# A decoder layer on one core: the weights' rounding in pieces of 768 columns, one to a batch, and single operations on x placed one step apart

## The chip, the cores and the metric

The kernel runs on one core of one Trainium2 chip. The core has five engines, each with its own queue of instructions that it works off in order: PE (TensorE, matrix products and transposes), DVE (VectorE), ACT (ScalarE), POOL (GpSimd) and SP (SyncE, which here only issues DMAs). The engines wait for one another by semaphores that are written out in the kernel. The metric is the device time of one execution in microseconds (us), as the median of three.

## The reference

One decoder layer over x of 16 batches x 256 rows x 512 columns, in three parts that each normalise x and add to it:

```python
x = x + attention(layernorm(x), w_qkv, w_proj)       # 16 heads of 32, causal
x = x + mixing(layernorm(x), k, bias, ctx, ctx, 8)   # long convolution along the 512 columns
x = x + ffn(layernorm(x), gate_w, up_w, down_w, ...) # 512 -> 1536 -> 512, silu(gate) * up

def bitlinear(x, w):       # in attention, for q, k, v and for the output
    xq = round(x * 127 / rowmax(|x|)), clipped to -128..127, times rowmax(|x|) / 127
    wq = round(w / mean(|w|)), clipped to -1..1, times mean(|w|)
    return xq @ wq.T

def quantized_matmul(x, w, scale):   # in the ffn
    return (x @ w.astype(float8_e4m3fn).astype(float32)) * scale
```

The change lies in the attention and in the rounding of gate_w and up_w (each 512 x 1536) to the values of the 8-bit format.

## The kernel before

The program has two parts. Part 1 does the attention of all 16 batches and writes x + attention to a scratch tensor in memory; beside it, it rounds gate_w and up_w and writes them as float16 to another one, `wq8_dram`. Part 2 does mixing and ffn, and is not touched but for the form in which it reads `wq8_dram`. It starts when both scratch tensors are complete (`part1_done`).

Part 1 has no planner. Each engine's program runs one loop over the same **steps** t (`STEPS`, from -13 to 153), and in a step it issues what `pair`, `batches`, `project_steps`, `halves` and `weight_step` give for that t. A step takes one **pair** of heads: 8 pairs to a batch (`PAIRS`), so a batch takes 8 steps, and everything that a batch needs once comes back every 8 steps. This text calls t mod 8 the **phase** of a step. In step t there are:

- PE: `weigh` of pair t-12 (probabilities times v), `row_max` of pair t (scores into the PSUM tile `s_qk`), `probabilities` of pair t-8 (scores, turned, into `s_kq`), and once or more a batch `turn_oq`, `project_out`, `multiply_qk`, `multiply_v`, `turn_xq`, `spread_c`, `turn_max`;
- DVE: `take_max` of pair t-1 (maxima from `s_qk`, tile blockmax), and the rest of a batch: scaling of q and k (`qkt`), splitting of v (`vHL`), norm statistics, row maxima, `finish`;
- ACT: `weighed` of pair t-13 (tile oraw), `exponentials` of pair t-9 (pT), `high_part` of pair t-10 (pH, the float16 rounding; at phase 2 DVE does it), and a batch's normalising, rounding, copies and diagonals;
- POOL: `low_part` of pair t-11 (pL), `low_qk`, small things, and two of the four operations on a piece of weights.

`s_qk` and `s_kq` exist once, so `row_max` of pair t waits for `take_max` of pair t-1, and `probabilities` waits for the exponentials of the pair before. pT and pH have three buffers, pL two. The results of all other products go to three PSUM banks in turn (`misc1`, class `Banks`): who takes a bank waits until the one taken three before has been released.

What a batch needs once is placed by numbers: `batches(t, FINISH, 13)` gives k = 0 at phase 5, and k = 4 (phase 1) rounds both halves of the output `o_sb` on ACT, k = 5, 6 turn them on PE, k = 6, 7 copy them on ACT, k = 9, 11 project them on PE (phases 6 and 0), k = 10, 12 add them to x on DVE (phases 7 and 1). `batches(t, NORM_AT, ...)` with k = LOAD_AHEAD + j falls on phase j: x is normalised at 3, both halves rounded and both diagonals `diag` made at 6, all turned by PE at 7, all copied by ACT (`xqT`) at 0, and the diagonals' product copied (`cbc`) at 2.

A **piece** of weights is 128 rows x 512 columns, 24 in all. Its chain: SP loads it (fw_raw), DVE masks the exponent's bits out of it (fw_pow) and clamps that from below, ACT scales fw_pow, POOL adds fw_pow to fw_raw and later subtracts it again (fw_out, float16), SP stores fw_out. It is placed by a list of its own with a period of five steps:

```python
weight_steps = {t: i for i, t in enumerate(t for t in STEPS if t >= 0 and t % 5 < 2)}
```

so at t mod 5 = 1 DVE has mask and clamp and POOL the subtraction for the piece before, at t mod 5 = 0 POOL has the addition, and ACT scales two steps behind DVE. Phases and weights thus meet in a pattern that comes back every 40 steps.

Of the kernel before, what the change touches and what calls it, by code (L numbers as in the profile page):

```python
# [5 lines left out]
F32 = mybir.dt.float32  # L6
# [7 lines left out]
P = 128  # L14
# [52 lines left out]
def decoder_kernel(nc, x, skip, ctx_in, w_qkv, w_proj, k_turned, w_gate, w_up, w_down,  # L67
# [18 lines left out]
    PIECE = 512  # L86
# [4 lines left out]
    with ExitStack() as ctx:  # L91
# [18 lines left out]
        wmax = sb(ctx, "wmax", [P, 2, CB * INNER // PIECE], F32)  # L110
# [143 lines left out]
        fw_in, fw_stored = signals("fw_in", 3), signals("fw_stored", 2)  # L254
        fw_pow_done, fw_scaled, fw_added, fw_taken = signal("fw_pow"), signal("fw_scaled"), signal("fw_added"), signal("fw_taken")
# [27 lines left out]

        def pair(t, lag):
            n = t - lag
            return n if 0 <= n < B * PAIRS else None
# [24 lines left out]
        def weight_step(t):  # L311
            k = weight_steps.get(t)
            return k if k is not None and k < W_STEPS else None

        W_REST = range(min(len(weight_steps), W_STEPS), W_STEPS)

# [34 lines left out]
        def part1_done(w):  # L351

            for t in range(NT):
                x1_stored(w, t)
            for n in range(PIECES - 2, PIECES):
                w.wait_ge(fw_stored[n % 2], 16 * (n // 2 + 1))
            w.wait_ge(fw_pow_done, PIECES)
            w.wait_ge(fw_taken, PIECES)
# [32 lines left out]
        def tensor_program(tensor):  # L391
# [27 lines left out]
            def turn_xq(b):  # L419
                w.wait_ge(xround_done, b + 1)  # L420
                for j in range(2):
                    bank = misc1.take(("xqT", b, j), w, (xqT_done, 2 * b + j + 1))
                    for i in range(2):
                        cb = 2 * j + i
                        for t in range(NT):
                            made = T.transpose(bank[:, i * N + t * P:i * N + (t + 1) * P], xn[:, t, cb * P:(cb + 1) * P], ident[:])
                    made.then_inc(xqT_pe, 1)
# [86 lines left out]
            def turn_oq(b, j):  # L514
                w.wait_ge(o_round, b + 1)
# [26 lines left out]
            turn_xq(0)  # L542
# [7 lines left out]
            turn_xq(1)  # L550
# [4 lines left out]
            for t in STEPS:  # L555
# [6 lines left out]
                for b, k in batches(t, FINISH, 13):  # L562
                    if k in (5, 6):
                        turn_oq(b, k - 5)
                    if k in (9, 11):
                        project_out(b, (k - 9) // 2)
                for b, k in project_steps(t):
                    if k < 4:
                        multiply_qk(b, k)
                    elif k in (PAIRS + 5, PAIRS + 7):  # L570
                        multiply_v(b, (k - PAIRS - 5) // 2)
                for b, k in batches(t, NORM_AT, 11 + LOAD_AHEAD, 2):
                    if k == LOAD_AHEAD + 7:
                        turn_xq(b)
# [131 lines left out]
        def vector_program(vector):  # L706
# [109 lines left out]
            def finish(b, k):  # L816
# [23 lines left out]
                elif k in (10, 12):  # L840
                    t, xs = (k - 10) // 2, x_sb[b % NX]
# [5 lines left out]
            def weight_pieces(k):  # L847
                if k == 0:
                    return
                n, second = divmod(k - 1, 2)  # L850
                if not second and n < PIECES:

                    raw, pw = fw_raw[n % 3], fw_pow[n % 2]
                    wT_ready(w, 3)
                    w.wait_ge(fw_in[n % 3], 16 * (n // 3 + 1))
                    if n >= 2:
                        w.wait_ge(fw_taken, n - 1)
                    m, at = divmod(n, PIECES // 2)
# [927 lines left out]
```

## Time and profile before

| | before |
|---|---|
| time, median of 3 executions (lowest, highest) | 1638.09 us (1636.88, 1639.48) |
| the profiled execution: its time, its span | 1636.98 us, 1635.2 us |
| share of the span busy: PE, DVE, ACT, POOL | 91%, 78%, 43%, 61% |
| first and last `take_max` of part 1 (DVE) | 67.25 and 480.82 us |
| last addition to x in part 1 (DVE) | starts at 518.82 us |
| first work on part 2's x (DVE) | starts at 523.86 us |

The span goes from the first to the last instruction in the profile of one execution; the 1.8 us between it and that execution's time lie outside. Busy shares over the whole span mix two parts with different limits, so they say little on part 1. What happens in part 1 is read in windows of time, and a step's length is the distance from one `take_max` on DVE (line 790) to the next, since each step has exactly one.

### The profile page before, as it was taken

The page shows a single profiled execution, that of the slowest core. Times are in us where ns is not written, and L with a number is a line of the kernel's source. Part 1 is how long each engine was busy: PE and PEld are TensorE (multiplying, and loading weights), DVE is VectorE, ACT ScalarE, POOL GpSimd, SP SyncE. Part 2 cuts the span into 40 slices and gives each one's busy share as a digit, 9 for nine tenths or more (in the row PEclk, how much of TensorE's full clock was granted, in tenths as well). Part 3 has the DMA queues.
Part 4 walks back from the last instruction along what each step waited for, and adds up shares of the span by engine and source line. Part 5 has one row for each costly group of instructions (what it writes and reads, how often), then busy time and mean ns, then how long its engine had stood idle before and what let it go on. Part 6 is the DMA issues. An engine that isn't in the chain of part 4 may idle for free.

```text
span 1635.2 us, 24145 instructions
## 1 busy us (share of the span) xinstructions
PE 1492.7 (91%) x9045; PEld 841.9 (51%) x9045; DVE 1280.3 (78%) x1865; ACT 698.3 (43%) x1230; POOL 993.3 (61%) x722
## 2 busy tenths in 40 slices
PE   2589898988985978899999999999999999999998
PEld 2477777777763433444444444444444444444443
DVE  6689898999874879887788788878887878778621
ACT  4589898988884102322222222232223222222131
POOL 2379898998883366754664546645654565465242
PEclk9799999999997989999999999999999999999999
DMA  3544645454423322000200210030020020010010
GB/s 132 153 123 130 159 123 139 137 142 124 130 83 105 95 65 77 20 26 7 72 25 2 55 43 7 20 78 7 13 78 14 8 71 26 2 45 0 1 27 26
DMA packets 62036, 105.79 MB, mean 65 GB/s; under 512 B 7880, under 2 KB 14176, under 8 KB 61920
## 3 DMA queue, kind: packets, MB, share of 16 engines
q1 hardware_dynamic: 61728, 104.10, 23.4%
q8 instruction: 72, 1.18, 0.3%
q14 instruction: 44, 0.36, 0.1%
q10 hardware_dynamic: 192, 0.14, 0.1%
HBM read 50.74 MB, written 19.92 MB: 43 GB/s over the span
## 4 chain that ended last, share of the span: by engine, by line
PE 60%; DVE 4%; POOL 2%; issue 1%; ACT 0%; POOLq 0%; DVEq 0%
PE gu L663 20%; PE y L628 10%; PE gu L677 10%; PE y L631 3%; PE y L635 3%; PE y L632 3%; PE y L634 3%; PE y L636 3%; PE gu L616 3%; PE misc L643 1%; PE misc L653 1%; PE misc L592 1%; PE misc L536 1%; DVE z L975 1%; DVE oT L986 1%
## 5 line engine op out<-in xcount | busy, mean ns | idle before, releaser
L1548 POOL TENSOR_TENSOR fuL<-fu,fuH 128x512 f16<-128x512 f32 x96 | 125.1, 1303 | 248.1 <-ACT fuH L1355 248.1
L628 PE MATMUL y<-kv,toep 128*128 128x512 f32 x496 | 242.8, 612 | 19.9 <-DVE z L975 17.7
L1450 POOL TENSOR_TENSOR pL<-pT,pH 128x768 f16<-128x768 f32 x128 | 220.5, 1725 | 42.5 <-ACT pH L1197 25.7
L986 DVE TENSOR_REDUCE oT<-z 128x64 f32<-128x512 f32 x256 | 175.7, 686 | 8.8
L663 PE MATMUL gu<-fT,wg 128*128 128x512 f16 x768 | 181.5, 379 | 0.4 <-ACT fT L1374 0.4
L663 PE MATMUL gu<-fT,wu 128*128 128x512 f16 x768 | 181.4, 379 | 0.0
L982 DVE TENSOR_TENSOR z<-z,cT 128x512 f32<-128x512 f32 x112 | 168.0, 1500 | 3.8
L1355 ACT ACTIVATE fuH<-fu 128x512 f16<-128x512 f32 x96 | 60.2, 627 | 255.1 <-DVE fu L1001 255.1
L979 DVE TENSOR_TENSOR z<-y,shared 128x512 f32<-128x512 f32 x112 | 76.9, 687 | 90.8 <-PE y L632 76.9
L677 PE MATMUL gu<-wd,fuL 128*128 128x512 f16 x384 | 145.6, 379 | 0.0
L677 PE MATMUL gu<-wd,fuH 128*128 128x512 f16 x384 | 145.6, 379 | 0.0
L628 PEld LDWEIGHTS y<-kv,toep 128*128 128x128 f32 x496 | 92.8, 195 | 101.3 <-issue 62.0
L1516 POOL TENSOR_TENSOR kv<-vT,cT 128x1024 f32<-128x1024 f32 x64 | 138.5, 2183 | 5.5 <-ACT vT L1332 5.5
L1191 ACT ACTIVATE pT<-s_kq,ws 128x768 f32<-128x768 f32 x128 | 114.9, 898 | 51.9 <-PE s_kq L493 46.9
L663 PEld LDWEIGHTS gu<-fT,wg 128*128 128x128 f16 x768 | 75.1, 98 | 119.4 <-issue 47.1
L663 PEld LDWEIGHTS gu<-fT,wu 128*128 128x128 f16 x768 | 75.2, 98 | 106.4 <-issue 35.4
L790 DVE TENSOR_REDUCE blockmax<-s_qk 128x6 f32<-128x768 f32 x128 | 121.5, 949 | 9.8 <-PE s_qk L463 9.5
L975 DVE TENSOR_TENSOR z<-y,cT 128x512 f32<-128x512 f32 x144 | 98.4, 683 | 29.5 <-PE y L628 29.3
L1338 ACT ACTIVATE shared<-gu 128x512 f32<-128x512 f32 x56 | 33.4, 597 | 204.1 <-PE gu L616 204.1
L1443 POOL TENSOR_TENSOR qkhl<-qkt,qkhl 128x512 f16<-128x512 f32 x64 | 81.7, 1279 | 38.5 <-ACT qkhl L1177 38.5
L479 PE MATMUL s_kq<-pack 128*128 128x128 f16 x768 | 99.7, 220 | 0.0
L1001 DVE SCALAR_TENSOR_TENSOR fu<-gu,cols,sil 128x512 f32<-128x512 f32 x96 | 71.3, 743 | 33.6 <-PE gu L663 33.6
(188 smaller groups left out, 3433.9 us busy)
## 6 DMA issues: line engine op xcount, KB each, us to landing
pack<-qkhl SPq DMA_DIRECT2D x256, 128.0 KB, 2.5
x_sb<-in_x SPq DMA_DIRECT2D x16, 512.0 KB, 4.9
c_sb<-in_ctx SPq DMA_DIRECT2D x32, 256.0 KB, 4.6
hankel<-in_L_xattn_k SPq DMA_DIRECT2D x32, 256.0 KB, 4.2
x_grp<-x_scratch SPq DMA_DIRECT2D x32, 256.0 KB, 4.0
out_y<-yo SPq DMA_DIRECT2D x32, 256.0 KB, 2.9
x_scratch<-x_sb SPq DMA_DIRECT2D x15, 512.0 KB, 2.8
wraw<-in_L_attn_w_qkv SPq DMA_DIRECT2D x3, 1024.0 KB, 9.7
```

Source lines behind the costliest of these rows:

```text
L479: T.matmul(to, pack[:, 1, r, g, key * P:(key + 1) * P], pack[:, 0, r, g, query * P:(query + 1) * P], start=first, stop=False)
L628: made = T.matmul(to, tap(h, lb - kb), keys_values(h, kb, half), start=kb == 0, stop=kb == lb)
L663: made = T.matmul(bank[:], (wg, wu)[which][:, cb, ib * P:(ib + 1) * P], fT[:, cb, part, :], start=cb == 0 and part == 0, stop=cb == CB - 1 ...
L677: made = T.matmul(bank[:], src[:, ib, t * P:(t + 1) * P], wd[:, ib, :], start=ib == 0 and part == 0, stop=ib == IB - 1 and part == 1)
L790: V.tensor_reduce(out=blockmax[b % 2][:, p, :], in_=s_qk[:, 0:6, :], op=ALU.max, axis=AXIS.X, negate=True).then_inc(max_done, 1)
L975: V.tensor_tensor(z[n % 2][:], y, weight, ALU.mult).then_inc(m_zm, 1)
L982: chain.step(V.tensor_tensor(z[n % 2][:], z[n % 2][:], weight, ALU.mult))
L986: V.tensor_reduce(out=oT[h % 2][:, lb, own].rearrange("p (b j) -> p b j", b=HB), in_=z[n % 2][:], op=ALU.add, axis=AXIS.X).then_inc(m_z, 1)
L1191: S.activation(pT[n % NP][:], s_kq[:, 0:6, :], ACT.Exp, scale=ws[:, 4:5]).then_inc(exp_done, 1)
L1450: G.tensor_tensor(pL[n % 2][:], pT[n % NP][:], pH[n % NP][:], ALU.subtract).then_inc(low_done, 1)
L1516: G.tensor_tensor(kv[LB * (h % 2) + lb][:], vT[h % 2][:, lb, :].rearrange("p (b i) -> p b i", b=B).unsqueeze(2).broadcast_to([P, B, M_POS, ...
L1548: G.tensor_tensor(fuL[:, ib, :], fu[n % 2][:], fuH[:, ib, :], ALU.subtract).then_inc(f_fl, 1)
```

## The change

The pieces become 768 columns wide and 16 in number, one to a batch, and `weight_steps` goes: piece n is masked at t = 8n + 2, clamped at 8n + 3, scaled at 8n + 4, added at 8n + 11, subtracted at 8n + 12 and stored at 8n + 13, where piece n + 2 is loaded too. The mask and the clamp are joined by a semaphore of their own (`fw_mask`) and no longer by the chain inside one step. fw_raw has two buffers for three, fw_out one for two.

The operations on x that stood two in a step stand one in a step: the output's rounding at k = 4, 5, its turning at 6, 7, the copies at 7, 8, projecting at 10, 11, the addition to x at 11, 12; x's rounding at phases 6 and 7, its turning at 0 and 1, the copies at 1 and 2, the diagonals at 0. The number of these operations is the same; the signals `o_round` and `xround_done` count halves now.

```diff
-    PIECE = 512
+    PIECE = 768
...
-        fw_raw = [q(f"fw_raw{i}", [P, PIECE], F32) for i in range(3)]
+        fw_raw = [q(f"fw_raw{i}", [P, PIECE], F32) for i in range(2)]
...
-        fw_out = [q(f"fw_out{i}", [P, PIECE], F16) for i in range(2)]
+        fw_out = q("fw_out", [P, PIECE], F16)
...
+        OUT_ROUND_AT, OUT_TURN_AT, OUT_COPY_AT, OUT_AT, X1_AT = (4, 5), (6, 7), (7, 8), (10, 11), (11, 12)
+
+        X_ROUND_AT, X_TURN_AT, X_COPY_AT = (6, 7), (8, 9), (9, 10)
+
+        V_AT, V_SPLIT_AT = (13, 15), (14, 16)
...
-        weight_steps = {t: i for i, t in enumerate(t for t in STEPS if t >= 0 and t % 5 < 2)}
-        W_STEPS = 1 + 2 * (PIECES + 1)
...
+        MASK_AT, CLAMP_AT, FACTOR_AT, ADD_AT, TAKE_AT, STORE_AT = 2, 3, 4, 11, 12, 13
+
+        def piece(t, at):
+            n, k = divmod(t - at, PAIRS)
+            return n if k == 0 and 0 <= n < PIECES else None
...
-            def turn_xq(b):
-                w.wait_ge(xround_done, b + 1)
-                for j in range(2):
...
+            def turn_xq(b, j):
+                w.wait_ge(xround_done, NT * (b + 1))
...
-                for b, k in batches(t, FINISH, 13):
-                    if k in (5, 6):
-                        turn_oq(b, k - 5)
-                    if k in (9, 11):
-                        project_out(b, (k - 9) // 2)
+                for b, k in batches(t, FINISH, 14):
+                    if k in OUT_TURN_AT:
+                        turn_oq(b, OUT_TURN_AT.index(k))
+                    if k in OUT_AT:
+                        project_out(b, OUT_AT.index(k))
...
-                elif k in (10, 12):
-                    t, xs = (k - 10) // 2, x_sb[b % NX]
+                elif k in X1_AT:
+                    t, xs = X1_AT.index(k), x_sb[b % NX]
...
-            def weight_pieces(k):
...
+            def mask_piece(n):
+                wT_ready(w, 3)
+                w.wait_ge(fw_in[n % 2], 16 * (n // 2 + 1))
+                if n >= 2:
+                    w.wait_ge(fw_taken, n - 1)
+                V.tensor_scalar(fw_pow[n % 2][:].bitcast(I32), fw_raw[n % 2][:].bitcast(I32), EXPONENT, None,
+                                ALU.bitwise_and).then_inc(fw_mask, 1)
...
+            def take_piece(n):
+                w.wait_ge(fw_added, n + 1)
+                if n > 0:
+                    w.wait_ge(fw_stored, 16 * n)
+                G.tensor_tensor(fw_out[:], fw_raw[n % 2][:], fw_pow[n % 2][:], ALU.subtract).then_inc(fw_taken, 1)
...
-                    elif k == LOAD_AHEAD + 6:
-                        round_in(b)
-                    elif k == LOAD_AHEAD + 8:
-                        copy_xqT(b)
...
+                    for i in range(NT):
+                        if k == LOAD_AHEAD + X_ROUND_AT[i]:
+                            round_in(b, i)
+                    if k == LOAD_AHEAD + 8:
+                        diagonal(b)
+                    for j in range(2):
+                        if k == LOAD_AHEAD + X_COPY_AT[j]:
+                            copy_xqT(b, j)
...
+                if (n := piece(t, STORE_AT)) is not None:
+                    store_piece(n)
+                    load_piece(n + 2)
```

**ACT at phases 6 and 7** of a full batch, in the order of its queue. oraw opens a step; xn is the rounding of x, qkhl the high half of q and k, nmT the turned maxima. Before, in a batch where the weights' list meets phase 6:

```order
L1205 ACTIVATE oraw<-pv 128x2x130
L1191 ACTIVATE pT<-s_kq,ws 128x768
L1197 ACTIVATE pH<-pT 128x768
L1177 ACTIVATE qkhl<-qkt 128x512
L1137 ACTIVATE xn<-xn,small 128x512 x2
L1142 ACTIVATE diag<-ident,small 128x128 x2
L1184 ACTIVATE nmT<-misc 32x256
L1236 ACTIVATE fw_pow<-fw_pow 128x512
L1205 ACTIVATE oraw<-pv 128x2x130
L1191 ACTIVATE pT<-s_kq,ws 128x768
L1197 ACTIVATE pH<-pT 128x768
L1177 ACTIVATE qkhl<-qkt 128x512
```

The same two steps of the changed kernel (its line numbers are 6 to 10 higher):

```order
L1214 ACTIVATE oraw<-pv 128x2x130
L1200 ACTIVATE pT<-s_kq,ws 128x768
L1206 ACTIVATE pH<-pT 128x768
L1186 ACTIVATE qkhl<-qkt 128x512
L1143 ACTIVATE xn<-xn,small 128x512
L1193 ACTIVATE nmT<-misc 32x256
L1214 ACTIVATE oraw<-pv 128x2x130
L1200 ACTIVATE pT<-s_kq,ws 128x768
L1206 ACTIVATE pH<-pT 128x768
L1186 ACTIVATE qkhl<-qkt 128x512
L1143 ACTIVATE xn<-xn,small 128x512
```

One rounding has moved to phase 7, the diagonals to phase 0, the weights' scaling (which met phase 6 here by its period of five) to phase 4.

**ACT at phase 2**, with the end of phase 1 before it. osmall is a batch's output scale, cbc the spread scale of x. Before:

```order
L1218 ACTIVATE o_sb<-o_sb,osmall 128x512 x2
L1223 ACTIVATE osmall<-osmall,ws 128x2
L1113 ACTIVATE small<-small 128x2
L1114 ACTIVATE small<-small 128x2
L1205 ACTIVATE oraw<-pv 128x2x130
L1191 ACTIVATE pT<-s_kq,ws 128x768
L1149 ACTIVATE cbc<-misc 128x256
L1184 ACTIVATE nmT<-misc 32x256
```

The changed kernel, phase 2 alone:

```order
L1214 ACTIVATE oraw<-pv 128x2x130
L1200 ACTIVATE pT<-s_kq,ws 128x768
L1227 ACTIVATE o_sb<-o_sb,osmall 128x512
L1232 ACTIVATE osmall<-osmall,ws 128x2
L1166 ACTIVATE xqT<-misc 128x512
L1159 ACTIVATE cbc<-misc 128x256
L1193 ACTIVATE nmT<-misc 32x256
```

One rounding of the output, its scale and one copy of turned x have come into the step; the copy of the maxima nmT stands behind them.

**DVE at phases 1 and 2** (and 3). x_sb is the addition to x. Before, in a batch where the weights' list meets phase 1:

```order
L790 TENSOR_REDUCE blockmax<-s_qk 128x6
L844 SCALAR_TENSOR_TENSOR x_sb<-misc,osmall,x_sb 128x512
L780 TENSOR_SCALAR vHL<-misc,small 128x16x32
L783 SCALAR_TENSOR_TENSOR vHL<-misc,small,vHL 128x16x32
L859 TENSOR_SCALAR fw_pow<-fw_raw 128x512
L861 TENSOR_SCALAR fw_pow,wmax<-fw_pow 128x512
L790 TENSOR_REDUCE blockmax<-s_qk 128x6
L814 CAST pH<-pT 128x768
```

The changed kernel, phases 1 to 3 of every batch that has a piece:

```order
L800 TENSOR_REDUCE blockmax<-s_qk 128x6
L854 SCALAR_TENSOR_TENSOR x_sb<-misc,osmall,x_sb 128x512
L790 TENSOR_SCALAR vHL<-misc,small 128x16x32
L793 SCALAR_TENSOR_TENSOR vHL<-misc,small,vHL 128x16x32
L800 TENSOR_REDUCE blockmax<-s_qk 128x6
L824 CAST pH<-pT 128x768
L862 TENSOR_SCALAR fw_pow<-fw_raw 128x768
L800 TENSOR_REDUCE blockmax<-s_qk 128x6
L818 TENSOR_TENSOR nmT<-misc,nmT 32x256
L790 TENSOR_SCALAR vHL<-misc,small 128x16x32
L793 SCALAR_TENSOR_TENSOR vHL<-misc,small,vHL 128x16x32
L869 TENSOR_SCALAR fw_pow,wmax<-fw_pow 128x768
```

The mask stands behind the cast at phase 2 and the clamp a step later. The other addition to x, which stood at phase 7, stands at phase 0.

## Rows read from the trace of the kernel before

**Rows 1.** Stage windows: us, then each engine's busy us, clock, DMA share, GB/s.

```profile
490.00:545.00 55.00, 34.31 (x217) 18.14 (x218) 27.28 (x37) 21.86 (x40) 25.98 (x17) 0.78 0.49 144
```

**Rows 2.** Windows in part 1: PE, PEld, DVE, ACT, POOL busy, in this order.

```profile
162.12:300.65 138.53, 125.21 (x1521) 102.32 (x1520) 125.10 (x207) 123.16 (x244) 124.55 (x92) 0.99 0.52 138
274.90:300.65 25.75, 24.30 (x305) 20.14 (x304) 24.05 (x45) 24.13 (x49) 23.68 (x18) 1.00 0.56 155
241.10:247.06 5.96, 4.44 (x53) 3.06 (x51) 5.43 (x13) 5.96 (x13) 5.96 (x5) 1.00 0.00 1
```

**Rows 3.** Timeline of DVE, four starts of a step: start us, length us.

```profile
136.32 0.95 DVE L790 TENSOR_REDUCE blockmax<-s_qk 128x6 f32<-128x768 f32 x1
162.12 0.95 DVE L790 TENSOR_REDUCE blockmax<-s_qk 128x6 f32<-128x768 f32 x1
300.65 0.95 DVE L790 TENSOR_REDUCE blockmax<-s_qk 128x6 f32<-128x768 f32 x1
385.60 0.95 DVE L790 TENSOR_REDUCE blockmax<-s_qk 128x6 f32<-128x768 f32 x1
```

**Rows 4.** Groups by form in 162.12 to 300.65: busy, mean ns, idle before.

```profile
L1450 POOL TENSOR_TENSOR pL<-pT,pH 128x768 f16<-128x768 f32 x40 | 69.1, 1730 | 13.6 <-ACT pH L1197 8.4 <-PE pv L511 5.1
L790 DVE TENSOR_REDUCE blockmax<-s_qk 128x6 f32<-128x768 f32 x41 | 38.9, 949 | 2.0 <-PE s_qk L463 2.0
L1191 ACT ACTIVATE pT<-s_kq,ws 128x768 f32<-128x768 f32 x41 | 36.8, 897 | 15.9 <-PE s_kq L493 14.4 <-POOL pL L1450 1.2
L1197 ACT ACTIVATE pH<-pT 128x768 f16<-128x768 f32 x35 | 29.3, 838 | 0.0
L1443 POOL TENSOR_TENSOR qkhl<-qkt,qkhl 128x512 f16<-128x512 f32 x21 | 27.2, 1295 | 0.0
...
L1127 ACT ACTIVATE xn<-x_sb,small 128x512 f32<-128x512 f32 x10 | 7.6, 810 | 0.0
...
L844 DVE SCALAR_TENSOR_TENSOR x_sb<-misc,osmall,x_sb 128x512 f32<-128x512 f32 x10 | 7.5, 747 | 0.2
...
L1218 ACT ACTIVATE o_sb<-o_sb,osmall 128x512 f32<-128x512 f32 x10 | 6.6, 715 | 0.0
L1137 ACT ACTIVATE xn<-xn,small 128x512 f32<-128x512 f32 x10 | 6.6, 713 | 0.0
...
L1157 ACT ACTIVATE xqT<-misc 128x512 bf16<-128x512 f32 x10 | 5.3, 576 | 0.0
...
L808 DVE TENSOR_TENSOR nmT<-misc,nmT 32x256 bf16<-32x256 f32 x10 | 4.1, 413 | 2.2 <-ACT nmT L1184 2.0
...
L1142 ACT ACTIVATE diag<-ident,small 128x128 f32<-128x128 f32 x10 | 3.4, 390 | 0.0
```

**Rows 5.** The weights' operations, same view and window.

```profile
L1466 POOL TENSOR_TENSOR fw_out<-fw_raw,fw_pow 128x512 f16<-128x512 f32 x8 | 10.8, 1354 | 0.0
L1469 POOL TENSOR_TENSOR fw_raw<-fw_raw,fw_pow 128x512 f32<-128x512 f32 x8 | 10.2, 1271 | 0.0
L859 DVE TENSOR_SCALAR fw_pow<-fw_raw 128x512 int32<-128x512 int32 x8 | 8.5, 1062 | 0.0
...
L861 DVE TENSOR_SCALAR_CACHE_REDUCE fw_pow<-fw_pow 128x512 f32<-128x512 f32 x8 | 5.5, 686 | 0.3
...
L1236 ACT ACTIVATE fw_pow<-fw_pow 128x512 f32<-128x512 f32 x8 | 5.0, 622 | 0.0
```

**Rows 6.** Timeline of all engines at 244.44 to 244.52.

```profile
244.47 1.94 DVE L859 TENSOR_SCALAR fw_pow<-fw_raw 128x512 int32<-128x512 int32 x1
244.49 1.64 POOL L1450 TENSOR_TENSOR pL<-pT,pH 128x768 f16<-128x768 f32 x1
```

**Rows 7.** The mask's line over the whole run: ns min/median/max.

```profile
L859 DVE TENSOR_SCALAR fw_pow<-fw_raw x24: 414/903/1951, 70.1 to 448.7; 128x512 int32<-128x512 int32 x24
```

**Rows 8.** Timeline of PE, two neighbours of four products each.

```profile
300.26 1.03 PE L528 MATMUL misc<-wprojT,oqT 128*128 128x512 bf16 x4
301.12 1.03 PE L446 MATMUL misc<-wqkvT,xqT 128*128 128x512 bf16 x4
```

More of the change, by code:

```diff
@@ L549, in tensor_program @@
             spread_c(1)
-            turn_xq(1)
+            for j in range(2):
+                turn_xq(1, j)
             bank = misc1.take("tab", w, (tab_done, 1))
@@ L569, in tensor_program @@
                         multiply_qk(b, k)
[L570 to L574, printed above, removed]
+                    elif k in V_AT:
+                        multiply_v(b, V_AT.index(k))
+                for b, k in batches(t, NORM_AT, LOAD_AHEAD + 11, 2):
+                    for j in range(2):
+                        if k == LOAD_AHEAD + X_TURN_AT[j]:
+                            turn_xq(b, j)
                     if k == LOAD_AHEAD + 9:
@@ L845, in finish, with clamp_piece @@
                                            in1=xs[:, t, :], op0=ALU.mult, op1=ALU.add).then_inc(x1_done, 1)
-            def weight_pieces(k):
[L848 to L858, printed above, removed]
-                    chain.step(V.tensor_scalar(pw[:].bitcast(I32), raw[:].bitcast(I32), EXPONENT, None, ALU.bitwise_and))
-                    chain.wait()
-                    V.tensor_scalar(pw[:], pw[:], FP8_MIN_NORMAL, None, ALU.max, ALU.max,
-                                    accum_out=wmax[:, m, at:at + 1]).then_inc(fw_pow_done, 1)
+            def mask_piece(n):
[5 more added lines that the diff above has]
+                                ALU.bitwise_and).then_inc(fw_mask, 1)
+            def clamp_piece(n):
+                m, at = divmod(n, PIECES // 2)
+                w.wait_ge(fw_mask, n + 1)
+                V.tensor_scalar(fw_pow[n % 2][:], fw_pow[n % 2][:], FP8_MIN_NORMAL, None, ALU.max, ALU.max,
+                                accum_out=wmax[:, m, at:at + 1]).then_inc(fw_pow_done, 1)
             stats_in(0)
@@ L902, in vector_program @@
                     high_part(n)
-                for b, k in batches(t, FINISH, 13):
+                for b, k in batches(t, FINISH, 14):
                     finish(b, k)
@@ L919, in vector_program @@
                         join_max(use)
-                if (k := weight_step(t)) is not None:
-                    weight_pieces(k)
-            for k in W_REST:
-                weight_pieces(k)
+                if (n := piece(t, MASK_AT)) is not None:
+                    mask_piece(n)
+                if (n := piece(t, CLAMP_AT)) is not None:
+                    clamp_piece(n)
             scored(w)
@@ L1261, in scalar_program @@
             copy_c(0)
-            copy_xqT(0)
+            for j in range(2):
+                copy_xqT(0, j)
             copy_weights(1)
@@ L1271, in scalar_program @@
             step_in(1)
-            round_in(1)
+            for i in range(NT):
+                round_in(1, i)
+            diagonal(1)
             copy_weights(3)
             copy_c(1)
-            copy_xqT(1)
+            for j in range(2):
+                copy_xqT(1, j)
             for t in STEPS:
@@ L1283, in scalar_program @@
                     high_part(n)
-                for b, k in batches(t, FINISH, 13):
+                for b, k in batches(t, FINISH, 14):
                     finish(b, k)
@@ L1304, in scalar_program @@
                         high_max(use)
-                if (k := weight_step(t - 2)) is not None and k > 0:
-                    weight_pieces(k)
+                if (n := piece(t, FACTOR_AT)) is not None:
+                    scale_piece(n)
                 if t == PREFETCHED_AT:
@@ L1681, in sync_program @@
             for t in STEPS:
-                for b, k in batches(t, FINISH, 13):
-                    if b == B - 1 and k in (10, 12):
-                        store_half((k - 10) // 2)
-                    elif k == 12:
+                for b, k in batches(t, FINISH, 14):
+                    if b == B - 1 and k in X1_AT:
+                        store_half(X1_AT.index(k))
+                    elif k == X1_AT[1]:
                         store_x1(b)
```

158 lines of the change are left out of this document (67 added, 91 removed).

## The prediction

> **What bounds the kernel now.** Part 2 is the same instructions in both kernels, so I read part 1. In the stage windows of steady state [rows 2] 40 steps, one full period of phases and weights, take 138.53 us, and no engine is the bound by itself: PE is busy 125.2, DVE 125.1, POOL 124.6, ACT 123.2 us. The two starts 40 steps apart [rows 3] say the same: a batch of 8 steps lasts 27.7 us and holds 25.0 us of each engine. The missing 2.7 us are waits that go round: the groups with idle time before them [rows 4] show pL on POOL waiting for ACT and PE (13.6 us), pT on ACT for PE (15.9), and each is the first instruction of its step. The reason is in the code: one `s_qk`, one `s_kq` and three pT let no engine run more than about a step ahead of another. So a step lasts about as long as its busiest engine, and it is not always the same one. The window of one step, 241.10 to 247.06 [rows 2], took 5.96 us with ACT and POOL busy throughout, where a mean step takes 3.46.
>
> **Loads by phase.** I added the durations of what each engine has in each phase, from the groups by form [rows 4, 5] and their neighbours in that view. Instructions overlap a little with the next (the groups' sums exceed the busy time of [rows 2]); I took off 0.09 us each on ACT, 0.06 on DVE, 0.045 on POOL. For PE the two neighbours [rows 8] start 0.86 us apart: I took 0.9 for each product of a batch of this size (v, projecting, one of four for q and k), 0.5 for four transposes, and 1.8 for the three things of every step as the rest. An example, ACT phase 6: pT 0.897, pH 0.838, oraw 0.375, qkhl 0.621, roundings 2 x 0.713, diagonals 2 x 0.390, nmT 0.358 make 5.30, less 9 x 0.09 is 4.49, and a fifth of the weights' scaling (0.53) makes 4.59. Without a rounding and the diagonals it is 3.26. Us per step, before > after, weights spread over the phases before and in their places after:
>
> | phase | DVE | ACT | POOL | PE |
> |---|---|---|---|---|
> | 0 | 3.09 > 3.44 | 3.55 > 3.07 | 3.44 > 2.94 | 3.6 > 4.1 |
> | 1 | 3.30 > 2.96 | 3.69 > 3.25 | 3.44 > 2.94 | 2.7 > 3.2 |
> | 2 | 1.93 > 2.78 | 1.76 > 2.96 | 3.22 > 2.71 | 3.2 > 2.7 |
> | 3 | 2.97 > 3.60 | 3.89 > 3.28 | 2.19 > 3.34 | 3.2 > 3.2 |
> | 4 | 3.25 > 2.91 | 2.45 > 3.10 | 2.19 > 3.37 | 2.7 > 3.2 |
> | 5 | 3.17 > 2.83 | 2.60 > 3.00 | 3.35 > 2.84 | 3.0 > 3.0 |
> | 6 | 3.29 > 2.95 | 4.59 > 3.26 | 3.44 > 2.94 | 3.6 > 2.7 |
> | 7 | 4.05 > 3.02 | 2.48 > 2.99 | 3.44 > 2.94 | 2.8 > 2.7 |
> | batch | 25.0 > 24.5 | 25.0 > 24.9 | 24.7 > 24.0 | 24.8 > 24.8 |
>
> The batch sums before lie within 0.4 us of a fifth of [rows 2].
>
> **The change part by part.** (1) *Pieces of 768*: 24 become 16 with the same columns. From [rows 5], POOL pays 24 x (1.354 + 1.271) = 63.0 us before; 768 columns in the same form cost 1.73 (pL in [rows 4]), so 16 x (1.73 + 1.70) = 54.9 after. The scaling on ACT goes from 24 x 0.53 to 16 x 0.75 (pH, 768 columns, 0.838 less overlap): 12.8 to 12.0. The clamp goes from 0.69 + 0.08 to 0.96 + 0.08 (256 columns more, at the 0.27 us by which pT exceeds qkhl). (2) *The mask* is the unknown. It takes 0.414 to 1.951 us, mean 1.06 [rows 5, 7]; it took 1.94 where POOL began its pL 0.02 us later [rows 6]. Alone, 768 columns cost 0.414 x 1.5 = 0.62; behind one whole pL 0.62 + 1.73 = 2.35. I keep the mean's excess (0.65) and take 1.26. (3) *The moves* cost nothing in busy time: the same ten of each form in five batches [rows 4]. What is late next: q and k need both xqT copies, now at phases 1 and 2 before `multiply_qk` at 3; the second addition stays at phase 1; x's load and store keep their steps. (4) *Banks*: I followed the takes. Before, v at phase 0 waited for ACT's copy that ends phase 0 and v at 2 for cbc that ends ACT's phase 2; after, cbc's product at phase 1 waits for DVE's v split that ends its phase 1 (2.96 us), where PE stands at 1.8 + 0.5, and v at phase 2 for the second xqT copy. Waits of some tenths on both sides; I charge none. (5) *SP* issues 32 DMAs for pieces instead of 48, at a phase with no packing of q and k, and a load has five steps (16 us) to land. With 0.52 of the DMA engines' time used [rows 2] nothing is late. Two raw buffers serve as well as three: a piece is subtracted (phase 4) one step before its buffer is loaded again.
>
> A rule of the Trainium skill bears on (2). SBUF — State Buffer, section "Who interferes with whom", says that VectorE's `tensor_scalar` and cast in their two-port mode and any GpSimd instruction exclude each other for a whole instruction. [Rows 6] agree: the mask ends 0.28 us after POOL's pL does. By that rule, with POOL busy 93% of the time after, a mask would wait half a POOL instruction nearly always, some 1.4 us for 1.26: 2 us more in 16 pieces.
>
> **The sum.** If every step took its busiest engine, a batch would take 31.0 us before (over the 40 steps, weights in place) and 26.6 after. If the slack is one step, the busiest mean of two neighbouring steps counts: 28.35 before, 26.06 after. Measured are 27.7, which is 0.80 of the way from the bare 25.04 to 28.35. The same place after is 24.90 + 0.80 x 1.16 = 25.8. Nine full batches stand between the starts at 136.32 and 385.60 [rows 3], 249.3 us: 9 x (27.70 - 25.83) = 16.8 us. The other seven lack parts of the work and spread less badly; I give them 0.45 us each, 3 us. The drain at the end of part 1 (PE busy 34 of 55 us [rows 1]) is a chain of single operations of the last batch, in which two roundings in one step or two make no difference, and the last piece is stored at step 133, before x's last addition at 153: 0. Together 20 us: 1637.0 becomes 1617.0, and since the median of the runs stands 1.1 us above the profiled execution, 1618.
>
> That the even batch is near the truth shows in the trace: the batch from 274.90 to 300.65 has the same work and 1.6 pieces like the others, and took 25.75 us [rows 2].
>
> **Rivals.** *Waits take the place (0.17).* ACT's phase 2 grows from 1.76 to 2.96 and its nmT copy stands last; DVE's L808 at phase 3 needs it and already waits 2.0 us for it in ten [rows 4]. PE's phase 0 becomes the longest of all, 4.1 for 3.6. If 0.6 and 0.5 us come on top, a batch takes 26.9: 9 x 0.8 + 2 = 9 us, 1629. Against it: at phase 7, where ACT's phase 6 was 4.59, the same wait gets shorter.
> *Nearly no waits left (0.12).* A batch at the bare 24.9: 9 x 2.8 + 6 = 31 us, 1607. The 2.7 us that are lost now speak against all of it going.
> *Only the saved instruction time counts (0.05).* If the waits come from latency between engines and not from uneven steps, and PE's unchanged sum carries on: 1638. The even batch of 25.75 speaks against it.
> *Slower (0.06).* Cast and mask both stand in DVE's phase 2. If each waits for a whole pL, phase 2 is 0.89 + 2 x 2.29 = 5.5 us for 2.8. Its two pairs with phases 1 and 3 rise by 1.1 and 1.4, a batch takes 28.3, and the nine are 5 us slower: 1643. It decides from about 4.9 us in that phase on. For it: masks of 1.94 occur. Against: that is the largest of 24, the median is 0.90. The skill's rule above makes it possible, since it lets a whole instruction block; it doesn't say how often.
>
> **How the numbers follow.** The forecast, 25.1 to 26.7 us a batch and so 1611 to 1627, has 0.60. Below it lies 1607 with 0.12, above it 1629 (0.17), 1638 (0.05), 1643 (0.06). The range 1607 to 1632 leaves out about half of the second case and all of the last two, 0.2 in all. Within 0.2% (3.3 us, what three executions can tell from no change) is the case of 1638 and a corner of 1629: faster 0.88, same 0.06, slower 0.06.
>
> **What would show it.** Forty steps from a `take_max` in the middle of part 1 take 129 us, and all batches from the fourth on take the same time within 0.3 us, with no step above 4.3 us. Part 1's last addition to x begins near 499, and from there to the end nothing changes by more than 1 us. The mask's mean is 1.1 to 1.5 us in 16 instances. ACT's pT waits for PE fall to a half. I am wrong if a batch stays above 26.9 us though steps are even (latency), if L808 waits over 0.5 us a time, or if the mask's mean exceeds 2 us.

## The result, and the profile after

The changed kernel takes 1601.74 us in the median of four executions (1601.21 to 1602.39), the kernel before 1637.49 us beside it. The ratio is 0.978, with a 95% interval of 0.9763 to 0.9797: 2.2% or 36 us faster. The forecast of 1618 had the direction, but its range (1607 to 1632) ended above the time.

The page of the changed kernel, for its span, its busy times and slices (the profiled execution took 1601.21 us):

```profile
span 1599.4 us, 23982 instructions
...
PE 1479.1 (92%) x8967; PEld 839.6 (52%) x9045; DVE 1261.7 (79%) x1841; ACT 697.4 (44%) x1222; POOL 992.7 (62%) x706
...
POOL 2389999999973477456545654655645654566242
```

POOL shows nine tenths and more in every slice from the fourth to the eleventh, and part 1 ends 35 us earlier, not quite a slice of 40 us. The windows that answer to [rows 2], the first over batches 3 to 11 (72 steps from the `take_max` of pair 24 to that of pair 96), the second over 40 steps:

```profile
131.16:355.02 223.86, 219.16 (x2692) 181.84 (x2735) 210.63 (x352) 219.06 (x433) 221.83 (x154) 1.00 0.55 150
205.78:330.21 124.43, 122.17 (x1497) 101.11 (x1521) 116.51 (x198) 121.52 (x241) 122.94 (x86) 1.00 0.55 152
```

These nine batches took 249.28 us before [rows 3] and take 223.86 now: 27.70 us a batch, then 24.87. Busy time per batch fell by 1.7 us on DVE and by 0.3 to 0.6 us on the others, and most of the idle time went: POOL is busy 98.8% of the 40 steps, where it was busy 90%. (A small part of the fall is less work in the window: 40 steps hold 3840 columns of weights now, 5 x 768, and held 8 x 512 = 4096.) The groups by form in the 40 steps, to be read against [rows 4] and [rows 5]:

```profile
L1465 POOL TENSOR_TENSOR pL<-pT,pH 128x768 f16<-128x768 f32 x41 | 68.3, 1666 | 1.1 <-PE pv L518 0.7
...
L1200 ACT ACTIVATE pT<-s_kq,ws 128x768 f32<-128x768 f32 x41 | 36.8, 897 | 2.9 <-PE s_kq L500 2.5
...
L1480 POOL TENSOR_TENSOR fw_out<-fw_raw,fw_pow 128x768 f16<-128x768 f32 x5 | 9.1, 1824 | 0.0
L1474 POOL TENSOR_TENSOR fw_raw<-fw_raw,fw_pow 128x768 f32<-128x768 f32 x5 | 9.1, 1819 | 0.0
...
L818 DVE TENSOR_TENSOR nmT<-misc,nmT 32x256 bf16<-32x256 f32 x10 | 4.1, 414 | 0.3
...
L862 DVE TENSOR_SCALAR fw_pow<-fw_raw 128x768 int32<-128x768 int32 x5 | 2.8, 554 | 0.0
```

pL's idle time before it is 1.1 us where it was 13.6, pT's 2.9 where it was 15.9. The row that stands out is the last: the mask of 768 columns takes 0.554 us, about half of what the mask of 512 columns took on average. Over the whole run it is the same (min, median, max):

```profile
L862 DVE TENSOR_SCALAR fw_pow<-fw_raw x16: 546/554/556, 68.8 to 430.6; 128x768 int32<-128x768 int32 x16
```

Batches 4 to 11 take 24.81 to 25.14 us each, with nearly the same eight step lengths every time, from 2.0 us (phase 2) to 4.1 us (phase 3). So the batches became even, the steps did not, but the longest of before had 5.96 us [rows 2].

Of the 35.8 us between the spans, 25.4 are these nine batches, 7.7 the others up to the last `take_max` (164.3 us before, 156.6 now), 1.6 lie ahead of the first `take_max`, and 1.1 behind the last one.

### The profile page after: what moved, and what is told of

It is laid out like the page before. It is cut to its first block, busy times and chain, and to the rows that moved or that the text cites. A ratio compares the mean times of both kernels' runs of the same rounds, so it can differ in the third digit from the quotient of the medians.

```text
span 1599.4 us, 23982 instructions
## 1 busy us (share of the span) xinstructions
PE 1479.1 (92%) x8967; PEld 839.6 (52%) x9045; DVE 1261.7 (79%) x1841; ACT 697.4 (44%) x1222; POOL 992.7 (62%) x706
## 4 chain that ended last, share of the span: by engine, by line
PE 61%; DVE 4%; POOL 2%; issue 1%; ACT 0%; POOLq 0%; DVEq 0%
PE gu L673 21%; PE y L638 10%; PE gu L687 10%; PE y L641 3%; PE y L646 3%; PE y L642 3%; PE gu L626 3%; PE y L645 3%; PE y L644 3%; PE misc L663 1%; PE misc L602 1%; PE misc L653 1%; PE misc L543 1%; DVE z L983 1%; DVE oT L994 1%
## 5 line engine op out<-in xcount | busy, mean ns | idle before, releaser
L1465 POOL TENSOR_TENSOR pL<-pT,pH 128x768 f16<-128x768 f32 x128 | 216.6, 1694 | 10.9 <-ACT pH L1206 4.7
L1370 ACT ACTIVATE fuH<-fu 128x512 f16<-128x512 f32 x96 | 60.3, 628 | 254.8 <-DVE fu L1009 254.8
L1458 POOL TENSOR_TENSOR qkhl<-qkt,qkhl 128x512 f16<-128x512 f32 x64 | 85.9, 1345 | 41.1 <-ACT qkhl L1186 41.1
```

The source lines that it names most:

```text
L1465: G.tensor_tensor(pL[n % 2][:], pT[n % NP][:], pH[n % NP][:], ALU.subtract).then_inc(low_done, 1)
```

## The experiments

Times of whole kernels scatter more from one series of executions to the next than within one: the changed kernel alone gave 1601.7 and then 1606.4 us. Its nine batches took 223.86 and 223.84 us. The difference lies behind the last `take_max`: from there to the end it is 1153.3 us in one profile and 1159.4 in the other, and 4.7 of these 6.1 us fall in the drain of part 1, up to the end of the last addition to x (38.3 and 43.0 us, at a granted clock of 0.87 and 0.73). Over all kernels here the drain takes 36 to 43 us and the rest of the span, part 2 with its start, 1114 to 1118. So I compare batches 3 to 11 (the window from pair 24 to pair 96, divided by nine) and give the time beside it. Each ratio is to executions of the kernel before that were taken with it.

The nine batches do not hold the same share of the weights in every kernel: 15 pieces of 512 or 10 of 768 (7680 columns) in before, x_only and period7, and 9 of 768 (6912 columns) in the kernels with a piece to a batch. So the table also has the time from the first to the last `take_max`, in which all pieces of all kernels lie.

| kernel | us, median | ratio (95%) | us a batch | first to last `take_max`, us | mask median us |
|---|---|---|---|---|---|
| before | 1637.49 | 1 | 27.70 | 413.6 | 0.90 |
| x_only | 1626.93 | 0.9932 (0.9914 to 0.9951) | 27.23 | 405.9 | 0.80 |
| period7 | 1623.45 | 0.9909 (0.9891 to 0.9927) | 27.00 | 404.1 | 0.97 |
| before_nomask | 1618.15 | 0.9878 (0.9863 to 0.9892) | 26.07 | 393.6 | none |
| pool_heavy | 1617.07 | 0.9866 (0.9849 to 0.9883) | 26.04 | 394.8 | 2.00 |
| period7_nomask | 1611.96 | 0.9838 (0.9822 to 0.9855) | 25.95 | 392.7 | none |
| pool_heavy_nomask | 1608.30 | 0.9826 (0.9809 to 0.9843) | 25.65 | 387.4 | none |
| mask_shift | 1611.12 | 0.9840 (0.9826 to 0.9855) | 25.30 | 388.1 | 0.76 |
| sum_on_dve | 1611.49 | 0.9844 (0.9829 to 0.9859) | 25.23 | 386.9 | 0.55 |
| no_add | 1602.83 | 0.9787 (0.9768 to 0.9806) | 25.19 | 383.0 | 0.55 |
| add_on_dve | 1609.15 | 0.9821 (0.9799 to 0.9843) | 25.17 | 386.4 | 0.55 |
| weights_only | 1612.12 | 0.9844 (0.9826 to 0.9863) | 25.15 | 385.9 | 0.55 |
| the changed kernel | 1601.74 | 0.978 (0.9763 to 0.9797) | 24.87 | 380.5 | 0.55 |
| after_again | 1606.39 | 0.9804 (0.9785 to 0.9823) | 24.87 | 380.9 | 0.55 |
| clamp_at_2 | 1603.50 | 0.9787 (0.9773 to 0.9802) | 24.87 | 379.7 | 0.55 |
| nomask | 1603.01 | 0.9792 (0.9775 to 0.9808) | 24.78 | 379.7 | none |
| no_scale | 1604.47 | 0.9797 (0.9778 to 0.9816) | 24.77 | 381.0 | 0.55 |

### The two halves of the change

weights_only puts the operations on x back:

```diff
-        OUT_ROUND_AT, OUT_TURN_AT, OUT_COPY_AT, OUT_AT, X1_AT = (4, 5), (6, 7), (7, 8), (10, 11), (11, 12)
-        X_ROUND_AT, X_TURN_AT, X_COPY_AT = (6, 7), (8, 9), (9, 10)
+        OUT_ROUND_AT, OUT_TURN_AT, OUT_COPY_AT, OUT_AT, X1_AT = (4, 4), (5, 6), (6, 7), (9, 11), (10, 12)
+        X_ROUND_AT, X_TURN_AT, X_COPY_AT = (6, 6), (7, 7), (8, 8)
...
-                    if k == LOAD_AHEAD + 8:
+                    if k == LOAD_AHEAD + 6:
                         diagonal(b)
```

> The changed kernel with the output's and x's roundings, turns, copies, diagonals and additions put back to their old steps; the weights stay in pieces of 768, one to a batch. Theory A (a step lasts as long as its busiest engine, averaged over two neighbouring steps, and what made the batch long was mostly the weights landing on steps that were already full): by the loads of the steps a full batch holds 26.4 us by pairs of steps, against 28.35 before and 26.1 in the changed kernel, so this kernel keeps nearly all of the gain: 25.0 to 25.6 us a batch, 1602 to 1612 us. Theory B (the two halves of the change are independent and each levels its own part): about half of the gain, 1616 to 1624 us, batches of 26.3 us.

x_only keeps those moves and has the weights' code and list of before (`PIECE = 512`, `weight_steps`, three and two buffers).

> The changed kernel with the weights as before (24 pieces of 512 columns, by the list with a period of five steps), and only the operations on x spread. Theory A: by pairs of steps a batch holds 28.4 us, as before, because pieces still land on full steps; 27.3 to 28 us a batch, 1630 to 1640 us, and steps of 5 us and more are still there. Theory B: half of the gain, 1616 to 1624 us.

Measured: weights_only 25.15 us a batch, x_only 27.23. Theory B falls: the weights carry 2.55 of the 2.83 us. Theory A was right on where the gain lies and a little off on x_only (its range began at 27.3 us and 1630), which gains 0.47 us a batch where it expected next to nothing. From the other side x's part is 25.15 - 24.87 = 0.28. Together the halves make 3.02, so they are nearly additive. From the first to the last `take_max` it is the same picture: 27.7 us for the weights and 7.7 for x, of 33.1.

### Place or size of the pieces

period7 has the pieces of the change every seven steps:

```diff
-        MASK_AT, CLAMP_AT, FACTOR_AT, ADD_AT, TAKE_AT, STORE_AT = 2, 3, 4, 11, 12, 13
+        MASK_AT, CLAMP_AT, FACTOR_AT, ADD_AT, TAKE_AT, STORE_AT = 2, 3, 4, 6, 7, 8
...
-            n, k = divmod(t - at, PAIRS)
+            n, k = divmod(t - at, 7)
```

> The changed kernel with its 16 pieces of 768 columns placed every 7 steps instead of every 8 (mask, clamp, scaling, addition, subtraction and store at 2, 3, 4, 6, 7, 8 of 7n), so that the pieces sweep over all phases of a batch. Size and number of the pieces are those of the change, only the place is not. Theory A (the place pays): a batch holds 28.8 us by pairs of steps, so most of the gain is lost, 26.8 to 28 us a batch on average with a pattern of 7 batches, 1622 to 1640 us, and the mask's mean is near 1.1 us again since it meets POOL's long instructions. Theory C (fewer and larger instructions pay): batches stay near 25 us, 1602 to 1608 us.

Measured: 27.00 us, within theory A's range; the mask has its long instances again (0.547 to 1.997 us). Size and number alone are worth 27.23 - 27.00 = 0.2 us a batch, the place 27.00 - 24.87 = 2.1. A part of the 2.1 is the tenth piece that period7 has in these nine batches, but the time from the first to the last `take_max`, with all pieces of each kernel in it, says the same: 1.9 us for size and number, 23.6 for the place. Theory C falls.

pool_heavy moves POOL's two operations to phases with a low half of q and k (`ADD_AT, TAKE_AT = 8, 9`).

> The changed kernel with POOL's addition and subtraction at phases 0 and 1, where POOL has a low half of q and k beside pL, instead of 3 and 4, where it has pL alone. Nothing else moves. Theory A: POOL's steps 0 and 1 hold 4.7 us, a batch 28.0 us by pairs of steps; 26 to 27.5 us a batch, 1615 to 1635 us. Theory D (POOL is the bound by its sum, 24.6 us busy of a batch's 24.8, and the place doesn't matter as long as the period is 8): 24.8 to 25.2 us a batch, 1601 to 1606 us.

Measured: 26.04 us, at the lower end of theory A's; D falls. But the reason is not only the full POOL steps, since the mask rose to a median of 2.0 us, at most 2.18. At 294.05 us it stands for 2.00 us, and POOL's pL began at 293.67 and took 1.96: POOL is now in a long instruction when the mask comes.

### The mask

To part the two I left out the mask, in four kernels. They round gate_w and up_w to other values, so they serve for the time alone:

```diff
-                V.tensor_scalar(fw_pow[n % 2][:].bitcast(I32), fw_raw[n % 2][:].bitcast(I32), EXPONENT, None,
-                                ALU.bitwise_and).then_inc(fw_mask, 1)
...
-                w.wait_ge(fw_mask, n + 1)
-                V.tensor_scalar(fw_pow[n % 2][:], fw_pow[n % 2][:], FP8_MIN_NORMAL, ...
+                V.tensor_scalar(fw_pow[n % 2][:], fw_raw[n % 2][:], FP8_MIN_NORMAL, ...
```

> The changed kernel without the mask; the clamp reads the raw piece instead. It leaves out the masking of the exponent, so the rounding of the gate and up weights is another. Control for the next kernel. DVE has 0.5 us less in phase 2 and is not the bound: theories E, G, H all expect 24.8 us a batch, 1599 to 1603 us.

> The kernel with POOL's addition and subtraction at phases 0 and 1, and without the mask (it leaves out the masking of the exponent, so the rounding of the gate and up weights is another). Theory A (two full POOL steps of 4.7 us cost what they exceed the others by): about 26 us a batch as with the mask, 1612 to 1617 us. Theory G (what cost there was the mask of 2.0 us, and the cast, held up by POOL in phase 2): 24.8 to 25.3 us a batch, 1601 to 1606 us. Both with the cast held up (0.3 us) as before.

Measured: nomask 24.78, pool_heavy_nomask 25.65. With the mask, the two differ by 1.17 us, without it by 0.87. So about three quarters of pool_heavy's loss stay without the mask, and a quarter is the mask. Theory G's 24.8 to 25.3 was too low, A's 26 too high. That the three quarters are all POOL's full steps is not shown: the cast at phase 2 takes 1.04 us in the median of pool_heavy_nomask and 0.55 in nomask, so a part of the 0.87 can be the cast held up.

> The kernel before without the masks of its 24 pieces (it leaves out the masking of the exponent, so the rounding of the gate and up weights is another). Theory G+ (what made the batches of before long was mainly DVE held up by POOL in the masks, 1.06 us each in the mean for 0.41 alone): 26.0 to 26.5 us a batch for 27.7, 1613 to 1623 us. Theory A (pieces that land on full steps of ACT and POOL, the mask being one part): the mask's own 1.5 x 1.0 us a batch is partly on the path: 26.8 to 27.3 us, 1624 to 1634 us.

This one decides the share in the kernel before. Its nine batches, 26.07 us each, and the first lines of the waits in them:

```profile
134.67:369.26 234.59, 222.68 (x2736) 180.73 (x2733) 212.34 (x354) 221.23 (x439) 225.84 (x166) 1.00 0.55 145
```

```profile
PEld s_qk L458 <- DVE blockmax L790: 9.7, 17, 1.0
PEld pv L510 <- issue: 9.6, 20, 0.8
ACT pT L1189 <- PE s_kq L493: 9.5, 14, 1.6
```

The batch falls by 1.63 us, the range of G+. The nine batches of before hold 15 masks of 17.5 us in all, 1.94 us a batch (a mean of 1.17; the 1.06 of [rows 5] is that of eight). So in the kernel before a mask cost 0.98 us on the path, five sixths of its length, hold-up included, though no engine was the bound by its sum. From the first to the last `take_max` it is the same: 20.0 us for 24 masks of 24.1 us. The same in period7_nomask:

> The kernel with pieces of 768 columns every 7 steps, without the masks (it leaves out the masking of the exponent, so the rounding of the gate and up weights is another). With masks its batches took 27.0 us. Theory G+: 25.0 to 25.5 us, 1605 to 1610 us. Theory A: 26.3 to 26.8 us, 1616 to 1622 us.

Measured 25.95 us, between both theories: 1.05 us less than period7, and 1.17 more than nomask at the regular place. From the first to the last `take_max` the two differences are 11.3 and 13.0 us. The second is the price of the irregular place with no mask in it; which operations collide there was not tried one by one.

mask_shift moves the mask one step ahead (`MASK_AT = 1`).

> The changed kernel with the mask of a piece at phase 1 instead of phase 2, behind the split of v; all else stays. At phase 2 POOL has only two small operations beside pL, at phase 1 pL and a low half. Theory G (the mask's 0.55 us in the changed kernel come from its place beside POOL's small operations; beside long ones it is held up): mask mean 1.2 to 2.2 us in 16, as in the kernel with POOL's work at phases 0 and 1 (median 2.0); DVE has 1.2 us to spare in a batch, so a batch gets 0.2 to 1.2 us longer, 1605 to 1618 us. Theory H (the mask is short because of its size and number): it stays 0.55 us and the time 1600 to 1603 us.

Measured: 25.30 us, in G's range of loss, but its reason fell for the most part: the mask's mean over all 16 is 0.92 us, not above 1.2. Four of them are long (1.95, 1.72, 1.70, 1.07, in the first full batch and the last three); the others take 0.55 to 0.77. What the waits show in the nine batches is another thing:

```profile
ACT pT L1200 <- PE s_kq L500: 8.9, 17, 1.2
PEld s_qk L465 <- DVE blockmax L800: 6.7, 18, 1.2
POOL pL L1465 <- DVE pH L824: 5.6, 9, 1.0
```

At phase 2 DVE makes the pH that POOL's pL needs. The mask ahead of it makes DVE's phase 1 3.65 us for 2.97, the pH comes late, and POOL waits for it once in each of the nine batches, 0.6 us on average, which it did not in the changed kernel. H, which expected no loss, falls as well.

### What ends a batch now

> The changed kernel unchanged, beside the kernels of this call: 1600 to 1604 us, 24.87 us a batch, all theories.

> The changed kernel with the clamp behind the mask at phase 2, where DVE's step is the shortest (2.02 us), instead of at phase 3, where it is the longest (4.07 us). Theory A (the longest steps cost): phases 2 and 3 become 3.0 and 3.2 us, their sum stays near 6.1; only what other engines lost by the uneven pair comes back, at most 0.3 us a batch: 1597 to 1602 us. Theory I (DVE and ACT need a light phase 2 to catch up, since PE's load is highest at phase 0): 0.1 to 0.5 us a batch slower, 1602 to 1608 us.

Measured: after_again has 24.87 us a batch as before (its 1606.4 us lie above the 1600 to 1604 expected, by the drain told above). In clamp_at_2 phases 2 and 3 became 2.80 and 2.89 us for 2.02 and 4.07, and a batch 24.87, the same to 0.01. Both theories' losses and gains stayed away: a long step on DVE is no loss if DVE waited anyway, so the lengths of steps on one engine don't tell what sets the batch. That left POOL, busy 221.83 of 223.86 us.

> The changed kernel with one operation of a batch moved from POOL to DVE: the sum of a batch's second half of weighed values (1.5 us on POOL, 0.76 on DVE by its twin) at phase 5. Theory E (after the change POOL's sum is the bound: it is busy 24.65 of a batch's 24.87 us): POOL falls to 23.1 us, the next are PE and ACT with 24.3, so a batch takes 24.4 to 24.6 us and the kernel 1596 to 1600 us. Theory F (the four engines are tied within a step and DVE's phase 5 grows from 2.8 to 3.5 us): nothing or a loss, 1602 to 1608 us.

Edit: `V.tensor_tensor(raw[:, 1, :, 0:D], ...)` with `o_sum` in DVE's `finish` at k = 0, and POOL's `sum_parts` gone. Measured: 25.23 us, 0.36 longer. Theory E falls, F's direction holds. Three more kernels took it up. no_add returns from `add_piece` before its instruction, `take_piece` waits for the scaling, and the scaling's factor is 1; no_scale does so with ACT's `scale_piece`; add_on_dve moves the addition to DVE's loop with `ADD_AT = 10`.

> The changed kernel without POOL's addition (1.82 us a batch), and with the scaling's factor 1. It leaves out the addition of the scaled power and with it the rounding of the gate and up weights. Theory E (POOL's busy time, 24.65 of 24.87 us a batch, is the bound): POOL falls to 22.8 us, the next are PE and ACT at 24.35, a batch takes 24.4 to 24.6 us. Theory J (a batch is held by the round trip between the engines, and POOL is full because it waits inside its instructions for DVE's reads): 24.8 us, no change.

> The changed kernel without ACT's scaling of a piece (0.76 us a batch). It leaves out the scaling and with it the rounding of the gate and up weights. Theory E: no change, 24.8 to 24.9 us a batch, since POOL keeps its work. Theory J: a small gain if ACT is in the round trip, 24.3 to 24.8 us.

> The changed kernel with the addition of a piece moved from POOL (1.82 us at phase 3) to DVE (some 0.9 us at phase 2, its shortest step, 2.02 us). Theory E: POOL 22.8, DVE 24.3, a batch 24.4 to 24.6 us, 3 to 4 us in all below the changed kernel. Theory J (two instructions that both read SBUF twice hold each other up, and DVE's gets longer than by its size): DVE's addition takes 1 us and more, POOL's pL beside it gets longer, a batch takes 24.8 to 25.3 us as with the other sum on DVE.

Measured: no_add 25.19 us. With 1.8 us of POOL's work simply gone, a batch is 0.32 us longer. no_scale 24.77, add_on_dve 25.17. Theory E is refuted, J holds in its main point: nothing is gained by less work on POOL. It did not expect the loss in no_add. (no_add and no_scale round the weights to other values, too.) Where it comes from can be read at phase 6, in the multiplication of the weighed values (L840, two inputs in SBUF). In the changed kernel:

```profile
296.35 1.50 DVE L840 TENSOR_TENSOR o_sb<-oraw,osmall 128x1024 f32<-128x1024 f32 x1
...
296.73 2.14 POOL L1458 TENSOR_TENSOR qkhl<-qkt,qkhl 128x512 f16<-128x512 f32 x1
```

DVE has begun, and POOL's next instruction, 1.16 us otherwise, takes 2.14. (DVE's own 1.50 hold some 0.3 us of waiting too: POOL's pL before it ran to 296.77.) In no_add, DVE and then POOL:

```profile
298.23 2.13 DVE L840 TENSOR_TENSOR o_sb<-oraw,osmall 128x1024 f32<-128x1024 f32 x1
```

```profile
298.12 1.15 POOL L1458 TENSOR_TENSOR qkhl<-qkt,qkhl 128x512 f16<-128x512 f32 x1
299.24 2.62 POOL L1465 TENSOR_TENSOR pL<-pT,pH 128x768 f16<-128x768 f32 x1
```

POOL, being early, began first; DVE pays (2.13, where its shortest instance in the changed kernel is 1.23), and then POOL's pL too (2.62 for 1.65). In no_add this step of DVE is 3.5 us where it was 2.9, and so it is in sum_on_dve and in add_on_dve, where L840's like takes 2.20 and 2.13 us. That the lost 0.3 us of all three are this order of starting is argued from these rows; no kernel here changed that order alone. The length of L840 alone can't be it: in no_scale it takes 1.89 to 2.18 us and the step 3.4, and its batches are the shortest, 24.77 us. What the three losing kernels share and no_scale and the changed kernel lack is the second hold, a pL of 2.63 us behind it in each of the nine batches (at most 1.81 in the other two). No version that does all the work beat the changed kernel's 24.87 us a batch; leaving out the mask or the scaling, 0.55 and 0.76 us of work, brought 0.1.

## Why the prediction was wrong in size

**What bounds the kernel** was right: four engines near 25 us of a batch of 27.7, uneven steps, and a gain in part 1 alone. Part 2 and the drain changed by no more than the scatter. The forecast of 20 us fell short of the 35.8 in three places: 8.6 us in the nine batches (16.8 for 25.4), 4.7 in the others (3 for 7.7), and 2.7 at the two ends (nothing for 1.6 and 1.1).

**The mask's price failed.** The step was part (2): "I keep the mean's excess (0.65) and take 1.26", as busy time of DVE, an engine with nothing special about it. Measured are 0.554, with no excess in any of 16. Its place decides. In the kernel before, 22 of 24 masks start while POOL is in an instruction, and every one of the 22 ends 0.27 to 0.30 us after that instruction does; the other two take 0.41 and 0.42. Two rows of before, POOL and DVE: pL ends at 348.44, the mask at 348.72.

```profile
345.81 2.63 POOL L1450 TENSOR_TENSOR pL<-pT,pH 128x768 f16<-128x768 f32 x1
347.45 1.27 DVE L859 TENSOR_SCALAR fw_pow<-fw_raw 128x512 int32<-128x512 int32 x1
```

With 768 columns the distance is 0.41 or 0.42 us in the 13 masks of period7 that are held. In the changed kernel the mask comes when POOL's two small operations of phase 2 (0.7 and 0.2 to 0.4 us) are over or just ending, and pL starts behind it and is the one that is held a little (1.81 for 1.65 in seven of the nine batches):

```profile
260.04 0.55 DVE L862 TENSOR_SCALAR fw_pow<-fw_raw 128x768 int32<-128x768 int32 x1
260.29 1.81 POOL L1465 TENSOR_TENSOR pL<-pT,pH 128x768 f16<-128x768 f32 x1 [0.65 <-PE pv L518]
```

The row of the mask at 244.47 [rows 6] had shown the mechanism (the mask there starts 0.02 us before pL and still loses to it, with POOL's subtraction ahead of pL running to 244.52), and I spread its mean over all places.

The size alone would have changed little: with 0.55 for 1.26 the forecast's table gives 25.99 us by pairs of steps for 26.06. What the sum had wrong is the path. The busiest mean of two neighbouring steps gives all masks of before 0.6 us a batch (28.35 with them, about 27.7 without, by the same table). before_nomask shows 1.63 us a batch, 14.7 us in the nine, and nomask shows 0.9 us for the masks of after (223.86 - 223.00). So what the masks cost on the path fell by 13.8 us of 25.4, more than half of the gain; the other 11.6 us stand between the two kernels without masks (234.59 - 223.00).

**The interpolation failed with it.** "The same place after is 24.90 + 0.80 x 1.16 = 25.8" carried over that the kernel loses four fifths of what pairs of steps allow. Measured is 24.87, the bare sum of my table's busiest engine, so the share is about nothing. That the two agree so closely is in part luck: the profile has ACT busy 24.34 us a batch and POOL 24.65, of which about 1 us is waiting inside its instructions. The 0.80 was no property of the kernel: without the masks, and with the pieces at the same steps, a batch stands at 26.07. Pairs of steps ordered period7, pool_heavy, weights_only and the change rightly (28.8, 28.0, 26.4, 26.1 against 27.0, 26.0, 25.15, 24.87), and with 28.4 they put x_only too high. As a rank it served, as a time it did not.

**The other batches** were given 3 us and brought 7.7 (164.3 to 156.6). Without its masks the kernel before needs 159.0 us for them, so 5.3 of the 7.7 were the price of masks here too, and the failed step is the same.

**The ends** were given nothing. Ahead of the first `take_max` the moves of x bring 2.1 us, of which scatter took 0.5 back. In the three kernels with x's operations at their old steps (before, before_nomask, weights_only) the first `take_max` starts 6.8 us after DVE's row maximum of x before it and waits 2.0 us for PE; in all fourteen profiles with the moves (the changed kernel's two among them) it starts 4.8 us after it and does not wait. In the kernel before, PE had to turn a whole batch of x, behind ACT's roundings, before it came to the first scores:

```profile
64.17 1.97 PE L426 MATMUL misc<-ident,xn 128*128 128x128 f32 x8 [5.00 <-ACT xn L1137]
65.93 0.63 PE L458 MATMUL s_qk<-pack 128*128 128x256 f16 x2
```

In the changed kernel the turning comes a step later, and these scores are done at 60.3 us. So "the moves cost nothing" was right for busy time, but they shorten the start. What stands before that row maximum scatters by 2 us over all kernels. The 1.1 us behind the last `take_max` lie within the scatter of the drain.

**Rivals.** "Nearly no waits left", 0.12, is what happened, at 24.9 us a batch; its 31 us had the nine batches right (25.2 for 25.4) and 6 us for all the rest, where 10.4 were measured. "Waits take the place": L808's like at phase 3 does not wait (0.3 us in ten). "Slower", by cast and mask held up at phase 2: cast 0.55, mask 0.55; pool_heavy is the kernel in which it came true in part (mask 2.0, cast 0.87 in the median), and there the mask cost 0.4 us a batch (26.04 with it, 25.65 without), not enough to lose. The rule of the Trainium skill that the prediction cites (SBUF — State Buffer, section "Who interferes with whom") agrees with the masks of before and period7 above. What the prediction worked out from it, 1.4 us in the mean, does not, because a fixed pattern repeats one case and never meets the average.

**Checks named beforehand.** Forty steps 124.4 us for 129 forecast. Batches 3 to 11 are equal within 0.33 us, for 0.3 forecast, but the forecast named all from the fourth on, and batches 12 to 14, which have less to do, take 23.0 to 24.2. No step of the nine is above 4.2 us: right. The last addition begins near 483.6 us (the last two take 1.61 us from 482.81), for 499 forecast; from there to the end it is 1115.8 us for 1116.4: right. The mask's mean: wrong. pT's waits for PE: 14.4 to 2.5 us, more than the half forecast.

## What to carry to other kernels

In a loop whose engines are tied within a step, give side work the period of the loop and choose its place by what the *other* engine of a shared resource does there: here the place was worth 23.6 us of part 1 and size and number 1.9. A mean duration with a wide spread (0.41 to 1.95) hides prices that depend on the place, and a fixed schedule will pay one of them every time; look at which one its place gets, and leave the operation out once to see what it costs on the path. An engine that is busy 99% need not be the bound: take work from it before believing so.

## What the runs showed of the hardware

That less work on POOL can lengthen the loop was not expected: DVE and POOL instructions that both read two tensors in SBUF held each other up, and the one that began later grew by 0.6 to 1.0 us. The Trainium skill states this in SBUF — State Buffer, section "Who interferes with whom": a VectorE instruction with two SBUF inputs contends with a GpSimd instruction that reads SBUF. The trace agrees, in both directions: 2.14 for 1.16 us on POOL, 2.13 for 1.23 to 1.50 on DVE. The busy time of POOL holds such waiting: in each of the nine batches of the changed kernel one low half of q and k takes 2.14 to 2.16 us for 1.16, which is 1.0 of POOL's 24.65 us.
